# Second attention of a two-block language-model tower: VectorE masks scaled scores in place, ScalarE copies the output, and the chunks are turned over four passes of six

## The reference, cut to what matters

```python
draft = jnp.einsum('bhqd,bhkd->bhqk', qr, kr)
draft = draft + jnp.where(causal_future, neg, 0.0)
num_remain = max(min(Sq, MIN_REMAIN), Sq - int(Sq * MASK_OUT))     # 128 of 1024 keys
_, draft_indices = jax.lax.top_k(draft, num_remain)
mask = jnp.full((B, H, Sq, Sq), neg, dtype)
mask = mask.at[b_idx, h_idx, s_idx, draft_indices].set(0.0)
mask = jnp.where(causal_future[None, None, :, :], neg, mask)
scores = jnp.einsum('bhqd,bhkd->bhqk', qr, kr) / np.sqrt(HD).astype(np.float32) + mask
attn = jax.nn.softmax(scores, axis=-1)
out = jnp.einsum('bhqk,bhkd->bhqd', attn, v)
```

## Time and profile before

| | |
|---|---|
| Time before, median of 3 runs | 4968.22 us (4965.84 to 4972.65) |
| The profiled execution: time, span | 4971.85 us, 4969.9 us |
| Busy PE, DVE, ACT, POOL | 4028.0 (81%), 3258.2 (66%), 2802.1 (56%), 570.6 (11%) us |
| L999, the mask matmuls | 2240, 283.2 us busy |
| L1369, DVE's output copies | 32, 1207 ns each |

### The profile page before, as it was taken

The page is one execution under the profiler, slowest core; times in us unless marked ns, Lnnn a source line. Parts: engine busy times, 40 slices in busy tenths (PEclk is TensorE's granted clock), DMA queues, the critical chain, the costliest instruction groups (busy, mean ns, idle before and its releaser), DMA issues. The chain is left out here.

```text
span 4969.9 us, 85458 instructions
## 1 busy us (share of the span) xinstructions
PE 4028.0 (81%) x25611; PEld 2331.5 (47%) x25752; DVE 3258.2 (66%) x9570; ACT 2802.1 (56%) x6546; POOL 570.6 (11%) x1877
## 2 busy tenths in 40 slices
PE   6998999999999989954777467766777777776899
PEld 2445766667444444422444234433444444443454
DVE  3555777777233345548877887887787888786244
ACT  1114777777000001147888588888888888887100
POOL 1000000000000000002122121221221221222000
PEclk8999999999999999976787677777877777777899
DMA  3326322222211113221111011111011111010542
GB/s 143 78 67 168 81 56 72 66 68 64 94 51 51 54 34 78 67 56 22 28 28 25 4 28 28 25 28 28 5 28 28 28 25 28 10 22 6 135 111 78
DMA packets 308441, 260.38 MB, mean 52 GB/s; under 512 B 188672, under 2 KB 242704, under 8 KB 307920
## 3 DMA queue, kind: packets, MB, share of 16 engines
q1 hardware_dynamic: 307376, 254.32, 20.1%
q0 software_dynamic: 544, 0.07, 0.0%
HBM read 176.21 MB, written 78.12 MB: 51 GB/s over the span
## 5 line engine op out<-in xcount | busy, mean ns | idle before, releaser
L1086 ACT ACTIVATE a_sign<-arena,a_state 128x384 fp8e4<-128x384 f32 (+5 forms) x1056 | 917.6, 870 | 88.6 <-DVE a_state L1259 50.2
L980 PE MATMUL a_ps_s<-k,q 128*128 128x512 bf16 (+3 forms) x1475 | 390.4, 397 | 401.5 <-DVE arena L1361 260.0
L992 PE MATMUL a_ps_t<-ident,arena 128*128 128x128 f32 x1584 | 343.6, 335 | 258.4 <-ACT a_probT L1054 244.4
L1054 ACT ACTIVATE a_probT<-a_ps_t 128x512 f32<-128x512 f32 (+3 forms) x768 | 363.9, 478 | 244.4 <-PE a_ps_t L999 238.9
L1086 ACT ACTIVATE a_sign<-a_third,a_state 128x384 fp8e4<-128x384 f32 (+2 forms) x480 | 417.2, 871 | 71.9 <-DVE a_state L1298 59.2
L738 ACT ACTIVATE a_prob<-a_x_neg,a_shift 128x640 f32<-128x640 f32 (+7 forms) x512 | 397.2, 776 | 90.0 <-DVE a_x_neg L781 63.4
L980 PEld LDWEIGHTS a_ps_s<-k,q 128*128 128x128 bf16 x1536 | 145.7, 115 | 560.9 <-DVE arena L1361 289.6
L781 DVE TENSOR_SCALAR_CACHE_REDUCE a_x_neg<-a_ps_s 128x640 f32<-128x640 f32 (+7 forms) x512 | 378.6, 751 | 41.9 <-PE a_ps_s L662 26.2
L677 PE MATMUL a_ps_t<-ident,a_prob 128*128 128x128 f32 x2304 | 365.0, 282 | 35.9 <-issue 16.3
L1309 DVE MAX8 a_nine<-a_below 128x8 f32<-128x256 f32 (+6 forms) x448 | 371.0, 828 | 34.4 <-issue 1.7
L1018 PE MATMUL a_ps_o<-a_probT,vals 128*64 128x128 f32 x4608 | 393.0, 316 | 0.0
(11 more groups left out here) (262 smaller groups left out, 7169.3 us busy)
## 6 DMA issues: line engine op xcount, KB each, us to landing
q<-qk SPq DMA_DIRECT2D x256, 256.0 KB, 4.6
qk<-p_qkT SPq DMA_DIRECT2D x32, 960.0 KB, 6.2
h_rows<-h SPq DMA_DIRECT2D x32, 512.0 KB, 6.8
k<-qk SPq DMA_DIRECT2D x256, 64.0 KB, 4.9
h<-tok_h SPq DMA_DIRECT2D x16, 512.0 KB, 4.0
arena<-in_wo SPq DMA_DIRECT2D x16, 512.0 KB, 6.4
o<-a_o SPq DMA_DIRECT2D x16, 512.0 KB, 2.7
q<-o SPq DMA_DIRECT2D x16, 512.0 KB, 5.5
```

Source lines behind the costliest of these rows:

```text
L980: nc.tensor.matmul(score(n)[:, a:a + w], q[:, y, head, i * P:(i + 1) * P], k[:, y, a:a + w], start=(y == 0), stop=False, skip_group_check= ...
L992: nc.tensor.matmul(to[:, c:c + P], xs[old][:, at:at + P], ident[:, :], start=(c == 0), stop=False, is_transpose=True, skip_group_check=True)
L1054: nc.scalar.activation(probT[:, n % 4, 0:w], ps_t[:, (n + 1) % 2, 0:w], ACT.Exp).then_inc(probT_ready, 1)
L1086: ins = nc.scalar.activation(to, xs[mine][:, at:at + w], ACT.Sign, scale=-1.0, saturate=False, bias=state[:, par, 0, n:n + 1], accum_out=s ...
```

## The change

The mask no longer goes through PE. Scores are fetched times 2^-13 (`DOWN`), and `mark` replaces a tile in its own place by (score < limit) - score: minus the score where it is kept, one minus the score where it is not. ACT's exponential then takes a scale of -2^13, so that a masked entry comes to exp of about -8192. The row tops are no longer negated; the rows of the selector matrix for i = 0, which are not marked, carry the sign. The turn has no mask matmuls. The bf16 mask tile goes.

With marking in place the buffer that is marked is that of pair s - 1, and PE waits for one signal (`masked`) when all is marked. Twelve tiles are marked in pass 2, the last two in pass 3, and `exact_where_needed` follows these in pass 3, ahead of the fetches. The turning goes over four passes, six chunks in each, three between signs and three behind. DVE waits for turned rows under 3 in pass 2, under 6 in pass 3 and all in pass 4. Score tiles 8 to 11 move into PE's turn order. The output is copied by ACT behind pass 4, and PE waits for it after its first four turns. GpSimd loses one operation in `split_top`.

```diff
-        EARLY = {16: range(0, 4), 20: range(4, NARROW)}
+        EARLY = {12: range(0, 4), 16: range(4, NARROW), 20: range(NARROW, 10), 22: range(10, 12)}
+        rows_turned = [2 + max(n for n, m, i, a, w in CH if i < rows) for rows in (3, 6, TT)]
...
-                        mm = nc.tensor.matmul(to.rearrange(...), row_of[:, m * TT + i, :], topT..., start=False, stop=(i == 0), ...)
-                        for c in range(0, w if i else 0, P):
-                            at = ps_seg(m, i) + a + c
-                            mm = nc.tensor.matmul(to[:, c:c + P], mask[:, at:at + P], ident_b[:, :], start=False,
-                                                  stop=True, skip_group_check=True)
-                        mm.then_inc(turn_done, 1)
+                        nc.tensor.matmul(to.rearrange(...), row_of[:, m * TT + i, :], topT..., start=False, stop=True,
+                                         skip_group_check=True).then_inc(turn_done, 1)
...
-                        pe.wait_ge(mask_ready, (s - 2) * NS + NS)
-                        if not (isinstance(s, int) and s == 2):
-                            pe.wait_ge(o_ready, s - 2)
+                        pe.wait_ge(masked, s - 1)
...
+                            if n == 2 and not (isinstance(s, int) and s == 2):
+                                pe.wait_ge(o_ready, s - 2)
...
-                        for n in range(NARROW if st["value"] else 0, 2 * TT):
+                        for n in range(12 if st["value"] else 0, 2 * TT):
                             scores(n)
...
-                        nc.scalar.activation(probT[...], ps_t[...], ACT.Exp).then_inc(probT_ready, 1)
+                        nc.scalar.activation(probT[...], ps_t[...], ACT.Exp,
+                                             scale=(-1 if i else 1) / DOWN).then_inc(probT_ready, 1)
+                    def output():
+                        act.wait_ge(pv_done, (s - 2) * (NC // 2) + NC // 2)
+                        if not (isinstance(s, int) and s == 2):
+                            act.wait_ge(o_out, (s - 2) * 64)
+                        nc.scalar.copy(o[:, :], ps_o[:, :]).then_inc(o_ready, 1)
...
-                    EVAC_PASSES, LEFT = 3, 2
+                    EVAC_PASSES, LEFT = 4, 2
...
                         if p == EVAC_PASSES and st["keep"]:
                             top_evac()
+                        if p == PASSES - 1 and st["value"]:
+                            output()
...
-                        return nc.vector.tensor_scalar(mask[:, at:at + w], old_x[:, at:at + w], limit[:, r:r + 1], MASKED,
-                                                       ALU.is_lt, ALU.mult)
+                        nc.vector.scalar_tensor_tensor(out=old_x[:, at:at + w], in0=old_x[:, at:at + w],
+                                                       scalar=limit[:, r:r + 1], in1=old_x[:, at:at + w], op0=ALU.is_lt,
+                                                       op1=ALU.subtract)
...
-                        nc.vector.tensor_scalar(new_x[:, at:at + w], score(n)[:, 0:w], 1.0, None, ALU.mult, ALU.max,
+                        nc.vector.tensor_scalar(new_x[:, at:at + w], score(n)[:, 0:w], DOWN, None, ALU.mult, ALU.max,
...
-                    KEEPS = [n for n in range(NS) if RANKED[n][1] < HALF], [n for n in by_row if RANKED[n][1] >= HALF]
+                    KEEPS = range(0, NS - 2), (NS - 2, NS - 1)
...
-                        if p in (2, 3) and st["value"]:
-                            dve.wait_ge(turn_done, (s - 2) * TURNED + (half_turned if p == 2 else TURNED))
+                        if p >= 2 and st["value"]:
+                            dve.wait_ge(turn_done, (s - 2) * TURNED + rows_turned[p - 2])
...
                                 for n in MORE:
                                     fetch(n)
-                            if st["keep"]:
-                                if st["value"]:
-                                    dve.wait_ge(turn_done, (s - 2) * TURNED + wide_turned)
-                                for r in KEEPS[1][0:2]:
-                                    mark(r).then_inc(mask_ready, 1)
-                                exact_where_needed()
                             dve.drain()
                         if p == 3:
                             if st["keep"]:
-                                for r in KEEPS[1][2:]:
-                                    mark(r).then_inc(mask_ready, 1)
+                                for r in KEEPS[1]:
+                                    mark(r)
+                                exact_where_needed()
+                                dve.sem_inc(masked, 1)
...
-                        if p == 3 and st["value"]:
-                            output()
```

More of the change, by code:

```diff
@@ L846, in kept_attention @@
     RANKS = TT - 1
+    DOWN = 2.0 ** -13
     with ExitStack() as ctx:
@@ L856, in kept_attention @@
         xs = (arena[:, 0:2 * SEG], arena[:, 2 * SEG:4 * SEG], third[:, :])
-        mask = sb("mask", [P, 2 * SEG], BF16)
         probT = sb("probT", [P, 4, BANK])
@@ L891, in kept_attention @@
         TURNED, LOADED = NC + 1, 16 * 4
-        HALF, NARROW = 6, TT
-        EARLY = {16: range(0, 4), 20: range(4, NARROW)}
-        wide_turned = 2 + max(n for n, m, i, a, w in CH if i < HALF + 1)
-        half_turned = 2 + max(n for n, m, i, a, w in CH if i < HALF)
+        NARROW = TT
+        EARLY = {12: range(0, 4), 16: range(4, NARROW), 20: range(NARROW, 10), 22: range(10, 12)}
+        rows_turned = [2 + max(n for n, m, i, a, w in CH if i < rows) for rows in (3, 6, TT)]
         def score(n):
@@ L1195, in _ @@
                 nc.vector.memset(code[:, :], 0.0)
-                nc.vector.memset(floor[:, :], MASKED)
+                nc.vector.memset(floor[:, :], -MASKED * DOWN)
                 nc.vector.memset(marked[:, :], 0.0)
@@ L1204, in _ @@
                 nc.vector.tensor_tensor(rows[:, :], rows[:, :], of[2], ALU.add)
+                dve.drain()
+                for m in range(2):
+                    only = rows[:, m * TT:m * TT + 1]
+                    nc.vector.tensor_scalar(only, only, -1.0, None, ALU.mult)
                 dve.drain()
@@ L1246, in start @@
                         dve.drain()
-                        nc.vector.scalar_tensor_tensor(out=var[:, :], in0=stats[:, :, 2], scalar=1e-20, in1=stats[:, :, 5],
+                        nc.vector.scalar_tensor_tensor(out=var[:, :], in0=stats[:, :, 2], scalar=1e-28, in1=stats[:, :, 5],
                                                        op0=ALU.add, op1=ALU.add)
@@ L1334, in select_exactly @@
                         left, lost = below[:, 0, 0:w], below[:, 1, 0:w].bitcast(I32)
-                        nc.vector.tensor_copy(left, old_x[:, at:at + w])
+                        nc.vector.tensor_scalar(left, old_x[:, at:at + w], -1.0, None, ALU.mult)
                         dve.drain()
@@ L1360, in fetch @@
                         dve.wait_ge(s_done, (s + 1) * (2 * TT) + (n + 1))
-                        nc.vector.tensor_scalar(new_x[:, at:at + w], score(n)[:, 0:w], 1.0, None, ALU.mult, ALU.max,
+                        nc.vector.tensor_scalar(new_x[:, at:at + w], score(n)[:, 0:w], DOWN, None, ALU.mult, ALU.max,
                                                 accum_out=top[:, m * TT + i:m * TT + i + 1]).then_inc(x_ready, 1)
-                    def output():
-                        dve.wait_ge(pv_done, (s - 2) * (NC // 2) + NC // 2)
-                        if not (isinstance(s, int) and s == 2):
-                            dve.wait_ge(o_out, (s - 2) * 64)
-                        nc.vector.tensor_copy(o[:, :], ps_o[:, :]).then_inc(o_ready, 1)
                     def scale_first():
@@ L1388, in exact_where_needed @@
                                     select_exactly(n)
-                                    if n in KEEPS[0] or n in KEEPS[1][0:2]:
-                                        mark(n)
                                 dve.nop()
```

18 lines of the change are left out of this document (7 added, 11 removed).

## The result

The changed kernel takes 5117.7 us (median of 4 runs, 5113.5 to 5120.6) where the kernel before takes 4967.1: ratio 1.030, 95% interval 1.0282 to 1.0318. It is slower, as forecast, but by 150 us instead of 45, and outside the range. The profiled execution has a span of 5118.1 us against 4969.9; the mean granted clock is 0.818 against 0.865.

What follows compares the result with a forecast made beforehand. No engine was always busy; waits between DVE, ACT and PE set a 72.71 us slot. Passes summed to 74.5, + 1.8 us x 29 = + 52, less 8 outside: 5016 profiled, 5012 predicted, range 4905 to 5095.

Steps and rivals of the forecast that it cites:

- Marking: Pass 2 on DVE: twelve two-input marks take 8.1 us instead of 5.5; pass 2 becomes 15.0, a gain of 2.1.
- the changed constants: The new constants, with GpSimd's dropped operation, cost nothing, since they hang on no end.
- Evacs go from eight to six a pass: Pass 1: ACT's stream is shorter and starts on time, its 1.62 us of waiting go, 16.55 becomes 14.93.
- Output on ACT: The copy behind pass 4 delays stores and V's load; pass 0 loses 2.3 us in every second slot, 1.15 on average.
- GpSimd's wait: Pass 2: DVE's 1.88 us of waiting for GpSimd's limits, ahead of the later marks, goes.
- Pass 3: A new chain of DVE fetches and PE score tiles makes it 17.0 us, 17.35 with dear branches; loss 4.2.
- Rival B: Much slower: low clock all through pass 3, 19.35 us there and 13.1 in pass 4; 5122 us, chance 0.13.
- Outside the slots: The keep-only slot loses 2 us, the three last ones gain some 3, 0 and 7: - 8 together.
- A: Faster: pass 3's chain is no longer than ACT's own pass, 14.25 us; 4899 us, chance 0.23.
- C: A draw: full clock in pass 3, 15.35 us; 4954 us, or 4966 with marks at their upper bound; chance 0.17.
- the main case: Pass 3 partly at low clock, a slot of 74.5 us against 72.71; 5012 us, chance 0.47.

Runs made afterwards that it cites:

- e1: Changed kernel with PE's wait for V moved from the head of the slot to just ahead of the first values: 5088.1 us.
- e9: Kernel before with only the output copy moved from DVE to ACT, behind the signs of pass 3: 4962.2 us, ratio 0.9991.
- e4: Changed kernel with the mark as a one-input operation, so that the kept scores are lost: 5012.0 us.
- e3: Changed kernel with DOWN at 1 in place of 2^-13 and the small number on the variances at 1e-20: 5070.3 us.
- e10: Changed kernel with V wait at first values, fetches 6 and 7 ahead of pass 3's marks, three marks there, scale 2^-5: 4959.1 us.
- e12: Changed kernel with V wait at first values, fetches 6 and 7 first in pass 3, four marks there, scale 2^-5: 4956.8 us.
- e7: Changed kernel with the scores scaled by 2^-8 in place of 2^-13: 5119.9 us.
- e11: Changed kernel with V wait at first values, fetches 6 and 7 first and four marks in pass 3, scale 2^-13, small number 1e-20: 5005.8 us.
- e6: Changed kernel with twelve extra matmuls into a free bank ahead of score tile 9 in pass 3, to keep PE at work: 5088.0 us.
- e5: Kernel before with the mask matmuls taken out of its turns, so that nothing is masked: 4919.0 us, ratio 0.9902.
- e8: Changed kernel with V wait at first values, fetches 6 to 9 first and three marks in pass 3, score tiles 8 to 11 ahead of turn 20: 5076.5 us.

## Why the prediction was wrong in size

The sum put 44 us on the span and 148 came. Of the 104 that it lacked, about 40 lie in the plain slots (3.21 us each instead of 1.8), 50 in the second selecting slot, 7 in the first one, and 8 outside the slots. The direction was right, and the mechanism in part; two terms failed, "Marking" and the changed constants.

*What held.* "Evacs go from eight to six a pass": pass 1 was put at 14.93 and is 14.87. "Output on ACT": 1.15 us more in pass 0 forecast, 1.04 found, by the chain described, and e1 took it away; the near match is in part luck, since the wait cost about 3 us in eleven slots where I had 2.3 in every second one. The copy itself took 1005 ns. That it bought nothing in pass 3 is e9's.

*The step that failed most in the slots: "Marking".* Pass 2 was put at 15.0 and is 17.14. Three terms of it were too small, each read from one slot of 17.02 in the rows above. The twelve marks take 9.06 us, not 8.1; I had taken the nearest form (second input fp8, 1206 ns at 1024 columns), and two f32 inputs take 1278, and 482 at 256 instead of 418. That is the upper bound that I had named and not used. GpSimd's wait did not go: 0.46 us is left of it. And marking begins 2.89 us into the pass, not 2.3. Together that is 0.96 + 0.46 + 0.59 = 2.0. The terms themselves add up to 14.5, and 15.0 had room for PE's waits; against 14.5 another 0.4 is "issue" around fetches 4 and 5. Over 28 slots pass 2 is 55 us of the miss (its gain was put at 2.1 and is 0.15), and pass 4 gives 14 of them back. That the marks end the pass is e4's: with one input it is 14.65.

*The step that was missing: the second selecting slot.* "The changed constants: nothing, they hang on no end" was wrong by some 50 us. The thresholds are found by counting, and whether a tile must be selected exactly is decided by the data; I had taken a multiplication by a power of two as neutral to it. With scales 1 and 2^-5 one slot selects (e3, e10, e12), with 2^-8 and 2^-13 two (e7, and the change), with the same inputs; the small number isn't the cause (e11). Which step of the search comes out otherwise was not tried and stays open. One place to look is `inv_sqrt` (L81), which computes on the bits of the variance; that it is this one is not shown.

*Pass 3: the right sum from wrong terms, so luck.* 17.35 was forecast, 17.24 is the mean. To tile 9 I had 6.6 us and 0.35 for the slots with a dear branch; the mean of the plain slots is 5.6, since the branch costs 0.79 us of "issue" ahead of fetch 6 in the rows above (0.14 to 0.79 in the plain slots), not 1.85. From tile 9 to the end of tile 11 I had the mixed 6.6; the mean is 8.2, and the slot above, with 8.6, is at the figure of the low clock. Behind tile 11 I had 3.8; it is 3.5. Both figures for the stretch held: 8.6 at the low clock, and 4.75 in e6 at the full one, where 4.6 was forecast. That the nine slots of e6 take 15.05, where the forecast at full clock was 15.0, is luck again: the extra matmuls, and not the branch, start tile 9 late there. The rule that I cited of the Trainium skill, TensorE: Matmul & The Clock Gate (HAM oscillation), that waits between bursts cost the clock and that each burst pays anew, agrees here: PE waits 4.92 us and comes back low in the rows above, and the wait filled gives 1.00 in nine slots of 29. By it I had put pass 3 near 19.0; the slots at 0.71 have 17.6.

*Rival B had the price, not the cause.* 5122 was its time, with 5.6 us a slot from pass 3 at 19.35, pass 2 at 15.4 and pass 4 at 13.1. A slot grew by 3.2, pass 4 fell to 11.24, and 58 us come from the selecting slots.

*Outside the slots* I had put -8; it is nothing. *The chances:* by the parts that I named, A and half of C give 0.32 for faster, not 0.30, and the rest of the main case with B 0.55 for slower, not 0.57.

The accounts of a plain slot, forecast and found, against the earlier trace rows and the table: pass 0 +1.15 and +1.04, pass 1 -1.62 and -1.44, pass 2 -2.1 and -0.15, pass 3 +4.2 and +4.13, pass 4 +0.12 and -0.37.

## What to carry to other kernels

Moving work off a busy engine wins only what another engine waited for it: here that was 48 us (e5), and the marks' second input, the new chain between DVE and PE in pass 3, a late load and the second selecting slot cost more than that. Before a stream is reordered, follow the piece that is moved to the start of the next pass: e8 won 3.0 us in one pass and paid 3.9 in the next. And where data decides how much work is done, count that work before and after as one counts instructions; a change of scale is a change of data.
